# Output projection of 14 groups by Strassen's scheme, with its products behind the attention

## The chip, the cores and the metric
One core of one Trainium2 chip. The metric is the device time of one launch in microseconds; lower is better.

## The reference
```python
mod = (silu(c) @ wmod).reshape(4, 6, 1, -1)          # sa, ca, ga, sb, cb, gb; ga, gb kept away from 0
h = layernorm(x) * (1 + ca) + sa                     # x: 4 x 512 x 1024
q, k, v = rope(h @ wq), rope(h @ wk), h @ wv         # 32 query heads, 8 key heads, each 128
attn = softmax(window_256_causal(q k^T / sqrt(128))) # 4 query heads share a key head
x = x + ga * (attn @ v) @ wo                         # wo: 4096 x 1024
h = layernorm(x) * (1 + cb) + sb
x = x + gb * (sum over the top 2 of 8 experts: w_e * h @ A_e^T @ B_e^T)   # rank 64
```
All of it is float32. A product is made of three matmuls on numbers split in a high and a low part (hi*hi, hi*lo, lo*hi).

## The kernel before, in words
The work is cut into 32 groups n = 8b + g: a batch b of 512 tokens and one key head g with its four query heads. Tokens are taken in four tiles of 128. Phase 0 makes the modulation and the first normalisation, phase 1 the 32 groups, phase 2 the experts. `p1_pe` (L985) writes TensorE's order out by hand. One step of `pe_groups` (L995) does, for the group n-1, the attention (`pe_attention`, L888) and the output projection (`pe_wo`, L816), and then for group n the projections Q0 to Q3 and V (`pe_qv`, L933).

**The attention** goes through 16 units u (tile u // 4, head u % 4). A unit is a product of scores three units ahead, a transposition of the normalised probabilities (`pe_turn`, L859), and filler that covers the softmax on VectorE and ScalarE: one chunk (3 matmuls) of the next group's K at each of u = 0 to 7, and one whole half of the output projection (12 matmuls) behind u = 8, 10, 12 and 15. After u = 5, 9, 13 and the last come the values of a tile (`pe_values`, L867). For the last two tiles they read `vd` and a folded part of `pT`, which GpSimd makes (`pool_group`, L766): five operations for vd and one fold (L783) per unit from 8 on. **The output projection** has 8 halves per group (4 token tiles x 2 column halves of 512), each 4 heads x 3 matmuls; four run in the attention, four behind it. VectorE adds each to `acc` (`dve_wo`, L1261). Then come Q0 to Q3, 24 matmuls of 128x512 each, in banks 1 and 0 by turns; a bank is free when `dve_rope` (L1233) has read it. The rope of K and of each Q takes two copies on ScalarE, three operations on VectorE, a copy on ScalarE and a subtraction on VectorE.

**Batches.** In batch 0 the weights are split in high and low parts and kept in device memory; from batch 1 on SP fetches them (`sp_direct_group`, L533): w_q and w_v of group n once V of n-1 is done, w_k once K is done, w_o once the last half of n-1 is done. In the first four groups of batches 1 and 2 (below: turned groups) a tile of the next batch is normalised besides: statistics, a row stored and broadcast (`sp_turned_row`, L519), two multiplications on VectorE (L1434, L1436), ScalarE's `act_tile` (L1111) and `act_tile_hi`, VectorE's low part (L1447), and the store of both parts (`sp_tile_store`, L528, signals s_hst). These parts lie in the memory of pT, so `act_project` (L1082) ends with ScalarE's wait for that store ahead of the next attention:

```python
if tile is not None:
    eng.wait_ge(s_hst, 32 * (tile + 1))
```
Batch 3 splits the lora weights in its first four groups in the same way. All DMAs that matter here are issued by SP, in program order, onto one queue.

## Time and profile before
| | us |
|---|---|
| runs, lowest / median / highest | 2558.72 / 2559.74 / 2560.05 |
| the profiled execution | 2558.81 |
| its span | 2556.8 |
| TensorE, VectorE, ScalarE, GpSimd busy | 2532.4, 1609.7, 1112.4, 460.2 |
| DMA moved | 504.15 MB |

The span runs from the first to the last instruction; about 2 us of the execution lie around it. Busy times of TensorE overlap, since matmuls are pipelined: the distance from one start to the next says what one costs. The granted TensorE clock is 1.0 of full speed throughout.

### The profile page before, as it was taken

Reading aid. Unit: us, or ns where it says so; the run is one execution under the profiler, and the core shown is the slowest. Engines: PE = TensorE matmul, PEld = TensorE weight load, DVE = VectorE, ACT = ScalarE, POOL = GpSimd, SP = SyncE. Lnnn points to the kernel's source line nnn. Section 1 sums busy time; section 2 is a strip of 40 time slices with the busy share of each in tenths; the row PEclk is TensorE's granted clock in tenths of the full one; section 3 lists DMA queues with packets and bytes.
Section 4 is the critical chain, followed back from the end, with each engine's and each line's share of the span. In section 5 each row is a group of like instructions: output and inputs, shape, how many; then the busy total and the mean of one; then the engine's idle time right before and its main releaser. Section 6 shows DMA issues by size and latency. Waiting matters only on the chain.

```text
span 2556.8 us, 40925 instructions
## 1 busy us (share of the span) xinstructions
PE 2532.4 (99%) x12449; PEld 2101.0 (82%) x12449; DVE 1609.7 (63%) x4594; ACT 1112.4 (44%) x2585; POOL 460.2 (18%) x498
## 2 busy tenths in 40 slices
PE   7999999999999999999999999999999999999999
PEld 4888888887888888888888888888888888887887
DVE  6677776666666665556666665556666665556553
ACT  4555654443445443333445543333333443335441
POOL 0332233332111111102111110111111110101122
PEclk9999999999999999999999999999999999999999
DMA  8766676659445554347444554347554556446221
GB/s 339 280 222 241 246 271 224 244 179 374 171 158 190 199 183 151 117 149 298 167 167 166 197 183 164 137 148 267 189 204 175 203 201 228 180 170 261 101 83 58
DMA packets 160949, 504.15 MB, mean 197 GB/s; under 512 B 17552, under 2 KB 43984, under 8 KB 159312
## 3 DMA queue, kind: packets, MB, share of 16 engines
q1 hardware_dynamic: 156384, 486.65, 52.5%
q10 hardware_dynamic: 4464, 16.25, 1.7%
q8 instruction: 51, 0.84, 0.1%
q14 instruction: 50, 0.41, 0.0%
HBM read 381.17 MB, written 121.68 MB: 197 GB/s over the span
## 4 chain that ended last, share of the span: by engine, by line
PE 95%; DVE 2%; ACT 1%; DMA 1%; issue 1%; DVEq 0%; POOL 0%; ACTq 0%; SPq 0%; POOLq 0%
PE bank L788 30%; PE bank L790 29%; PE bank L789 29%; PE bank L864 4%; PE bank L853 1%; PE bank L1904 1%; PE bank L276 1%; PE bank L905 0%; DMA x1s<-x_scratch 0%; PE bank L303 0%; DMA wm<-in_wmod 0%; ACT w_o_hi L715 0%; PE bank L854 0%; PE bank L1955 0%; DVE qo_lo L1270 0%
## 5 line engine op out<-in xcount | busy, mean ns | idle before, releaser
L788 PE MATMUL bank<-w_o_hi,qo_hi 128*128 128x512 f32 x1024 | 411.4, 402 | 2.0 <-DVE qo_lo L1270 1.5
L790 PE MATMUL bank<-w_o_hi,qo_lo 128*128 128x512 f32 x1024 | 400.4, 391 | 0.0
L788 PE MATMUL bank<-hT_hi,w_q_hi 128*128 128x512 f32 x1024 | 399.5, 390 | 0.2 <-DVE swapped L1242 0.2
L789 PE MATMUL bank<-w_o_lo,qo_hi 128*128 128x512 f32 x1024 | 398.9, 390 | 0.0
L789 PE MATMUL bank<-hT_lo,w_q_hi 128*128 128x512 f32 x1024 | 398.5, 389 | 0.0
L790 PE MATMUL bank<-hT_hi,w_q_lo 128*128 128x512 f32 x1024 | 398.5, 389 | 0.0
L1050 ACT ACTIVATE prob<-prob,nbias 128x256 f32<-128x256 f32 (+1 forms) x512 | 247.3, 483 | 237.8 <-DVE nbias L1289 230.9
L783 POOL TENSOR_TENSOR pT<-pT,lower_t 128x256 fp32r<-128x256 f32 x256 | 196.0, 766 | 475.3 <-DVE pT L1323 475.3
L1241 DVE TENSOR_TENSOR rotated<-bank,cos_t 128x512 f32<-128x512 f32 x160 | 110.6, 692 | 261.8 <-ACT swapped L1035 261.1
L1265 DVE TENSOR_TENSOR acc<-bank,acc 128x512 f32<-128x512 f32 x256 | 173.7, 689 | 160.9 <-PE bank L790 160.8
L772 POOL TENSOR_TENSOR rotated<-v_all 128x256 f32<-128x256 f32 x64 | 48.1, 773 | 1231.5 <-DVE v_all L1329 1231.5
L1034 ACT ACTIVATE swapped<-bank 64x512 f32<-64x512 f32 x160 | 95.4, 596 | 360.4 <-PE bank L790 353.0
L1323 DVE TENSOR_TENSOR pT<-bank,pT 128x256 fp32r<-128x256 f32 (+1 forms) x512 | 195.7, 382 | 85.5 <-ACT pT L1147 85.3
L1147 ACT ACTIVATE pT<-bank 128x256 fp32r<-128x256 f32 (+1 forms) x512 | 177.5, 353 | 155.2 <-PE bank L864 150.2
L790 PEld LDWEIGHTS bank<-w_o_hi,qo_lo 128*128 128x128 f32 x1024 | 192.2, 188 | 42.2
L788 PEld LDWEIGHTS bank<-hT_hi,w_q_hi 128*128 128x128 f32 x1024 | 192.2, 188 | 42.0 <-issue 1.6
L788 PEld LDWEIGHTS bank<-w_o_hi,qo_hi 128*128 128x128 f32 x1024 | 192.3, 188 | 40.1 <-issue 3.2
L790 PEld LDWEIGHTS bank<-hT_hi,w_q_lo 128*128 128x128 f32 x1024 | 192.2, 188 | 40.0
L789 PEld LDWEIGHTS bank<-hT_lo,w_q_hi 128*128 128x128 f32 x1024 | 192.3, 188 | 39.6
L789 PEld LDWEIGHTS bank<-w_o_lo,qo_hi 128*128 128x128 f32 x1024 | 192.8, 188 | 36.7
L1289 DVE CUSTOM_DVE_ANT_0 prob<-bank,mask_t 128x256 f32<-128x256 f32 x384 | 162.4, 423 | 32.8 <-PE bank L864 10.9
L864 PE MATMUL bank<-ident_t,prob 128*128 128x128 f32 x896 | 177.1, 272 | 2.6 <-DVE prob L1299 2.1
(258 smaller groups left out, 4975.4 us busy)
## 6 DMA issues: line engine op xcount, KB each, us to landing
w_q_hi<-w_q_hi_scratch SPq DMA_DIRECT2D x96, 512.0 KB, 8.3
w_q_lo<-w_q_lo_scratch SPq DMA_DIRECT2D x96, 512.0 KB, 8.9
w_o_hi<-w_o_hi_scratch SPq DMA_DIRECT2D x96, 512.0 KB, 7.8
w_o_lo<-w_o_lo_scratch SPq DMA_DIRECT2D x96, 512.0 KB, 8.5
stage<-in_wq SPq DMA_DIRECT2D x32, 512.0 KB, 4.5
stage<-in_wo SPq DMA_DIRECT2D x32, 512.0 KB, 5.3
w_q_hi_scratch<-w_q_hi SPq DMA_DIRECT2D x32, 512.0 KB, 6.3
w_q_lo_scratch<-w_q_lo SPq DMA_DIRECT2D x32, 512.0 KB, 7.2
```

Source lines behind the costliest of these rows:

```text
L783: eng.tensor_tensor(pair[:, :, 2, :], pair[:, :, 0, :].bitcast(F32), lower_t[:].unsqueeze(1).broadcast_to([P, 2, P]), ALU.mult).then_inc(s ...
L788: eng.matmul(o, st[0], mv_[0], start=start, stop=False)
L789: eng.matmul(o, st[0], mv_[1], start=False, stop=False)
L790: return eng.matmul(o, st[1], mv_[0], start=False, stop=stop)
L864: m = eng.transpose(bank[5 + u % 2][:, b * P:(b + 1) * P], prob[:, u % GQ, b * P:(b + 1) * P], ident_t[:])
L1034: eng.activation(swapped[slot][0:half, :], bk[half:HD, :], ACT.Copy)
L1050: eng.activation(tile, tile, ACT.Exp, bias=nbias[:, u:u + 1], scale=-1.0, accum_out=rowsum[:, u:u + 1]).then_inc(s_exp, 1)
L1147: eng.activation(pT[i % 2][0][:, 0:nk, h * P:(h + 1) * P], bank[5 + u % 2][:, 0:nk * P].rearrange("p (b q) -> p b q", q=P), ACT.Copy).then ...
L1241: eng.tensor_tensor(rotated[slot][:], bk[:], cos_t[:], ALU.mult).then_inc(s_dve, 1)
L1265: eng.tensor_tensor(a, wo_bank(half)[:], a, ALU.add).then_inc(s_wor, 1)
L1289: plain(eng.tensor_tensor_reduce(prob[:, u % GQ, 0:w], SBANK[u % 3][:, 0:w], add, -SCALE, FAR, ALU.add, ALU.min, nbias[:, u:u + 1])).then_ ...
L1323: eng.tensor_tensor(lo, bank[5 + u % 2][:, 0:nk * P].rearrange("p (b q) -> p b q", q=P), hi.bitcast(F32), ALU.subtract).then_inc(s_ptl, 1)
```

## The change
In the first seven groups of batches 2 and 3 the output projection is made by Strassen's scheme. Tiles 0 and 1, and tiles 2 and 3, make a pair each. Of a pair the left matrix is 2 x 2 blocks (tile x two heads), the right one 2 x 2 blocks of w_o (two heads x 512 columns). Seven products M1 to M7, each 2 x 3 matmuls of 128x512, take the place of eight. GpSimd and ScalarE make the sums of the left blocks (ten per group, 128x256 each: a sum and a low part on GpSimd, a high part on ScalarE); VectorE adds or subtracts each product to one or two of the outputs (12 per pair). All products stand behind the attention: M3 and M4 of the first pair before its last values, the other twelve after them. In the attention, units 8 to 15 take one chunk each of Q0 of the next group.

The five sums of right blocks that aren't plain blocks of w_o are made once, in batch 1, by GpSimd (`pool_mix`): 28 pieces of 256 columns, each with its raw rows loaded and its two parts (640 KB each) stored by SP (`sp_mix_step`). Their tiles lie where the left sums lie later, so ScalarE waits for all stores before batch 2's attention. SP's fetches go by head (128 columns, pieces of 512 B) and by product, into places of w_q, w_k, w_v and w_o that come free. `plain_part` tiles keep attention outputs unsplit, probability tiles are narrower, and a scratch for DMAs shrinks from 8192 to 512. The diff, cut to its core:

```diff
+PAIRED = 2
+PAIRS = ((0, 1), (2, 3))
+ORDER = (3, 4, 1, 5, 2, 7, 6)
+OUTS = {3: ((0, 1, 1), (1, 1, 1)), 4: ((1, 0, 1), (0, 0, 1)), 1: ((1, 1, 1), (0, 0, 1)), 5: ((0, 1, 1), (0, 0, -1)),
+        2: ((1, 0, 1), (1, 1, -1)), 7: ((0, 0, 1),), 6: ((1, 1, 1),)}
+MIXED = (1, 3, 4, 6, 7)
+PIECES = 4
...
+        def head_slot(h):
+            return {0: (w_q, 0), 1: (w_k, None), 2: (w_q, 0), 3: (w_q, 2)}[h]
+        def mixed_slot(i):
+            return {3: (w_v, None), 4: (w_o, 0), 1: (w_o, 1), 5: (w_o, 2), 2: (w_o, 3), 7: (w_q, 4), 6: (w_q, 6)}[i]
...
+        def sp_enter(eng, n, b, mix=lambda i: None):
+            sp_fetch_qv(eng, n)
+            eng.wait_ge(s_proj, 6 * n + 2)
+            sp_fetch(eng, 5, (n + 1) % KV, s_dk)
+            mix(0)
+            eng.wait_ge(s_wo, wo_at(n, b) + 1)
+            for i in (4, 1, 5, 2):
+                sp_mixed(eng, i, n % KV)
+            mix(1)
+            mix(2)
+            eng.wait_ge(s_proj, 6 * n + 6)
+            sp_head(eng, 0, (n + 1) % KV)
+            sp_head(eng, 3, (n + 1) % KV)
+            for i in (7, 6):
+                sp_mixed(eng, i, n % KV)
+            mix(3)
+            eng.wait_ge(s_proj, 6 * n + 7)
+            sp_mixed(eng, 3, n % KV)
...
+        def sp_paired_group(eng, n, b, leave=False, before_v=lambda: None, before_q3=lambda: None):
+            m = n - 1
+            g = n % KV
+            eng.wait_ge(s_proj, 6 * n + 2)
+            sp_head(eng, 1, g)
+            eng.wait_ge(s_proj, 6 * n + 3)
+            sp_head(eng, 2, g)
+            before_v()
+            done = wo_at(m, b) + 1
+            eng.wait_ge(s_wo, done + len(ORDER) + ORDER.index(3) + 1)
+            sp_fetch(eng, 4, g, s_dv)
+            if leave:
+                eng.wait_ge(s_wo, wo_at(n, b) + 1)
+                for j in range(6, NC):
+                    sp_fetch(eng, j, g, s_do)
+            else:
+                for at, i in enumerate(ORDER):
+                    if i != 3:
+                        eng.wait_ge(s_wo, done + len(ORDER) + at + 1)
+                        sp_mixed(eng, i, g)
+            eng.wait_ge(s_proj, 6 * n + 4)
+                    if i != 3:
+                        eng.wait_ge(s_wo, done + len(ORDER) + at + 1)
+                        sp_mixed(eng, i, g)
...
+            if not leave:
+                eng.wait_ge(s_proj, 6 * n + 5)
+                sp_head(eng, 0, (n + 1) % KV)
+            before_q3()
+            if not leave:
+                eng.wait_ge(s_proj, 6 * n + 6)
+                sp_head(eng, 3, (n + 1) % KV)
+                eng.wait_ge(s_proj, 6 * n + 7)
+                sp_mixed(eng, 3, g)
+        def sp_mix_load(eng, piece):
...
+        def sp_mix(eng, first, pieces):
+            for at in range(len(pieces) - 1):
+                sp_mix_step(eng, first + at, pieces[at], pieces[at + 1])
+        def sp_mix_step(eng, at, piece, following):
+            eng.wait_ge(s_mix, 3 * at + 1)
+            if following is not None:
+                sp_mix_load(eng, following)
+            eng.wait_ge(s_mix, 3 * at + 3)
+            sp_mix_store(eng, piece)
...
+            if b < PAIRED:
+                def piece(i, g0=0):
+                    return g0 + i // PIECES, i % PIECES
+                sp_mix_load(eng, piece(0))
+                for t in range(QT):
+                    n = b * KV + 1 + t
+                    sp_turned_load(eng, b, t)
+                    sp_direct_group(eng, n, b, lambda: sp_turned_row(eng, b, t))
+                    sp_mix(eng, 3 * t, [piece(3 * t + i) for i in range(4)])
+                    sp_tile_store(eng, b, t)
+                with eng.Fori(1 + QT, KV) as g:
+                    sp_direct_group(eng, b * KV + g, b)
+                    sp_mix(eng, 4 * g - 8, [piece(i, g - 2) for i in range(5)])
+                return
...
+            with eng.Fori(1, 1 + QT) as g:
+                pool_group(eng, KV + g - 1)
+                for i in range(3):
+                    pool_mix(eng, 3 * g - 3 + i)
+            with eng.Fori(1 + QT, KV + 1) as g:
+                pool_group(eng, KV + g - 1)
+                for i in range(4):
+                    pool_mix(eng, 4 * g - 8 + i)
...
+        def pool_mix(eng, piece):
+            (b11, b12), (b21, b22) = ((r[:, 0, :], r[:, 1, :]) for r in raw)
+            lo = mix_lo[:].bitcast(F32)
+            eng.wait_ge(s_raw, WS_KEPT + 32 * piece + 32)
+            eng.wait_ge(s_mixd, WS_KEPT + 32 * piece)
+            eng.tensor_tensor(lo[:, 0, :], b11, b22, ALU.add)
+            eng.tensor_tensor(lo[:, 1, :], b12, b22, ALU.subtract)
+            eng.tensor_tensor(lo[:, 2, :], b21, b11, ALU.subtract)
+            eng.tensor_tensor(lo[:, 3, :], b11, b12, ALU.add)
+            eng.tensor_tensor(lo[:, 4, :], b21, b22, ALU.add).then_inc(s_mix, 1)
+            eng.wait_ge(s_mix, 3 * piece + 1)
+            plain(eng.tensor_copy(mix_hi[:], lo)).then_inc(s_mix, 1)
+            eng.wait_ge(s_mix, 3 * piece + 2)
+            eng.tensor_tensor(mix_lo[:], lo, mix_hi[:].bitcast(F32), ALU.subtract).then_inc(s_mix, 1)
...
+        def pe_product(eng, n, b, p, i):
+            t0, t1 = PAIRS[p]
+            if i == 3:
+                eng.wait_ge(s_ol, QT * n + 2 * p + 1)
+                left = sl(qo, lambda q: q[:, 0:2, t0 * P:(t0 + 1) * P])
+            elif i == 4:
+                eng.wait_ge(s_ol, QT * n + 2 * p + 2)
+                left = sl(qo, lambda q: q[:, 2:4, t1 * P:(t1 + 1) * P])
+                left = mixed_sum(p, i)[0:2]
...
+            if i in M_FREE[p]:
+                eng.wait_ge(s_wor, wor_at(n, b) + 1 + M_FREE[p][i])
+            elif p == 1 and i == 3:
+                eng.wait_ge(s_oh, oh_at(n, b) + HIGH_AT[1][22])
...
+                if u < KT:
+                    if u == 0:
+                        eng.wait_ge(s_dk, 32 * (n - (KV - 1)))
+                    m = mm3(eng, bank[0][:], sl(w_k, lambda t: t[:, u, :]), sl(hT, lambda t: t[:, u, :]), u == 0, u == KT - 1)
+                    if u == KT - 1:
+                        m.then_inc(s_proj, 1)
+                else:
+                    if u == KT:
+                        eng.wait_ge(s_dq[0], 32 * (n + 1 - (KV - 1)))
+                    m = pe_head_chunk(eng, 0, u - KT, 1)
+                    if u == UNITS - 1:
+                        m.then_inc(s_proj, 1)
...
+            pe_product(eng, n, b, 0, 3)
+            pe_product(eng, n, b, 0, 4)
+            pe_values(eng, n, b, QT - 1, True)
+        def pe_paired_group(eng, n, b, part=None):
+            pe_paired_attention(eng, n - 1, b)
+            for i in ORDER[2:]:
+                pe_product(eng, n - 1, b, 0, i)
+            for i in ORDER:
...
+            if r == 1 and b is not None:
+                eng.wait_ge(s_wo, wo_at(n, b) + 1)
...
+            if b == PAIRED:
+                eng.wait_ge(s_mixd, WS_KEPT + 32 * PIECES * (KV - 1))
...
+        def dve_product(eng, n, b, p, i):
+            eng.wait_ge(s_wo, wo_at(n, b) + 1 + len(ORDER) * p + ORDER.index(i) + 1)
+            for at, (t, c, sign) in enumerate(OUTS[i]):
+                after = sum_before(i, at)
+                if after:
+                    eng.wait_ge(s_wor, wor_at(n, b) + 1 + 12 * p + after)
+                a = acc[:, PAIRS[p][t], c * 512:(c + 1) * 512]
...
+        def dve_paired_group(eng, n, b, part=None, turned=None, g=None):
+            dve_attention(eng, n - 1, b, tile=turned, paired=True)
+            if turned is not None:
+                dve_turned_chain(eng, turned)
+            for i in ORDER[2:]:
+                dve_product(eng, n - 1, b, 0, i)
+            dve_rope(eng, n, 0)
+            for i in ORDER:
+                dve_product(eng, n - 1, b, 1, i)
             for r in range(1, 1 + GQ):
...
+                if turned is not None and r == 3:
+                    dve_tile_lo(eng, turned)
+                dve_rope(eng, n, r)
...
+                if turned is not None and r == 1:
+                    dve_turned_tile(eng, turned)
+                if g is not None and r == 1:
+                    dve_tile2(eng, g)
+                if g is not None and r in (2, 3):
+                    dve_lora_lo(eng, g, r - 2)
```

## Rows read from the trace of the kernel before
**Rows 1.** The page: busy time by engine, and the chain by engine.
```profile
PE 2532.4 (99%) x12449; PEld 2101.0 (82%) x12449; DVE 1609.7 (63%) x4594; ACT 1112.4 (44%) x2585; POOL 460.2 (18%) x498
...
PE 95%; DVE 2%; ACT 1%; DMA 1%; issue 1%; DVEq 0%; POOL 0%; ACTq 0%; SPq 0%; POOLq 0%
```
**Rows 2.** Waits of TensorE, 800 to 1450 us: total, times, longest.
```profile
PE bank L864 <- DVE prob L1299: 0.4, 1, 0.4
```
**Rows 3.** Timeline of TensorE, the output projection behind an attention: start, duration.
```profile
752.84 0.39 PE L788 MATMUL bank<-w_o_hi,qo_hi 128*128 128x512 f32 x1
...
763.49 0.39 PE L790 MATMUL bank<-w_o_hi,qo_lo 128*128 128x512 f32 x1
```
**Rows 4.** Timeline of TensorE: units 0 and 2, and vd of two attentions.
```profile
719.97 0.27 PE L864 MATMUL bank<-ident_t,prob 128*128 128x128 f32 x1
...
723.22 0.27 PE L864 MATMUL bank<-ident_t,prob 128*128 128x128 f32 x1
...
746.91 0.39 PE L788 MATMUL bank<-pT,vd 128*128 128x512 f32 x1
...
817.95 0.39 PE L788 MATMUL bank<-pT,vd 128*128 128x512 f32 x1
```
**Rows 5.** Groups of GpSimd by line and form: count, busy us, mean ns.
```profile
L720 POOL TENSOR_TENSOR w_q_lo<-stage,w_q_hi 128x1024 fp32r<-128x1024 f32 x28 | 66.7, 2400 | 23.8 <-ACT w_q_hi L715 23.8
...
L774 POOL TENSOR_TENSOR rotated<-rotated 128x256 f32<-128x256 f32 x32 | 23.7, 740 | 2.5
...
L776 POOL CAST vd<-rotated 128x256 fp32r<-128x256 f32 x32 | 12.7, 397 | 4.2
```
**Rows 6.** Timeline of GpSimd in the same group.
```profile
726.77 1.51 POOL L772 TENSOR_TENSOR rotated<-v_all 128x256 f32<-128x256 f32 x2 [46.96 <-DVE v_all L1329]
...
729.71 0.74 POOL L778 TENSOR_TENSOR vd<-rotated,vd 128x256 fp32r<-128x256 f32 x1
...
746.67 0.77 POOL L783 TENSOR_TENSOR pT<-pT,lower_t 128x256 fp32r<-128x256 f32 x1 [0.87 <-DVE pT L1323]
...
750.13 0.73 POOL L783 TENSOR_TENSOR pT<-pT,lower_t 128x256 fp32r<-128x256 f32 x1 [0.19 <-DVE pT L1323]
```
**Rows 7.** Timeline of SP's DMA issues in the same group.
```profile
763.91 0.33 SPq L508 DMA_DIRECT2D w_o_hi<-w_o_hi_scratch  x1
...
767.60 0.47 SPq L508 DMA_DIRECT2D w_o_lo<-w_o_lo_scratch  x1
782.66 0.53 SPq L531 DMA_DIRECT2D hT_hi_scratch<-l_hi  x1
783.23 0.68 SPq L531 DMA_DIRECT2D hT_lo_scratch<-l_lo  x1
```
**Rows 8.** DMA issues: count, KB each, median us to landing.
```profile
hT_lo_scratch<-l_lo SPq DMA_DIRECT2D x12, 512.0 KB, 5.6
...
lora_a_lo_scratch<-l_lo SPq DMA_DIRECT2D x2, 512.0 KB, 3.6
```
**Rows 9.** Stretches of 2 us; last columns: clock, DMA share, GB/s.
```profile
775.00:777.00 2.00, 2.00 (x10) 1.65 (x10) 0.94 (x2) 1.01 (x2) 0.00 (x0) 1.00 0.95 385
777.00:779.00 2.00, 2.00 (x11) 1.65 (x10) 1.27 (x3) 0.89 (x2) 0.00 (x0) 1.00 0.04 14
```
**Rows 10.** Timeline of ScalarE: the exponential of unit 2.
```profile
790.54 0.40 ACT L1050 ACTIVATE prob<-prob,nbias 128x128 f32<-128x128 f32 x1 [0.47 <-DVE nbias L1289]
```
**Rows 11.** Timeline of VectorE: the rope of K, and two sums.
```profile
755.52 0.69 DVE L1241 TENSOR_TENSOR rotated<-bank,cos_t 128x512 f32<-128x512 f32 x1
...
758.23 0.69 DVE L1257 TENSOR_TENSOR kt_all<-rotated,kt_all 128x512 fp32r<-128x512 f32 x1 [0.70 <-ACT kt_all L1044]
758.84 1.28 DVE L1265 TENSOR_TENSOR acc<-bank,acc 128x512 f32<-128x512 f32 x2
```
**Rows 12.** Timeline of TensorE in the opening: idle time before in brackets.
```profile
12.70 1.94 PE L303 MATMUL bank<-wm,cT 128*32 128x512 f32 x8 [6.12 <-DMA wm<-in_wmod]
...
27.75 1.93 PE L303 MATMUL bank<-wm,cT 128*32 128x512 f32 x16
```

More of the change, by code:

```diff
@@ new lines, in sp_mix_load, with sp_mix_store @@
+        def sp_mix_load(eng, piece):
+            g, jc = (piece[0], piece[1])
+            j, half = divmod(jc, 2)
+            for y in range(2):
+                rows = wo[bass.ds(g * GQ * HD + (j + 2 * y) * HD, HD), :].rearrange("p (c s n) -> p c s n", c=2, s=2)[:, :, half, :]
+                eng.dma_start(raw[y][:], rows).then_inc(s_raw, 16)
+        def sp_mix_store(eng, piece):
+            g, jc = piece
+            j, half = divmod(jc, 2)
+            for z, tile in enumerate((mix_hi, mix_lo)):
+                to = w_s[z][bass.ds(g * P, P), :].rearrange("p (i j s n) -> p i j s n", i=len(MIXED), j=2, s=2)[:, :, j, half, :]
+                eng.dma_start(to, tile[:].bitcast(F32)).then_inc(s_mixd, 16)
@@ L626, in x_tile @@
+            for g in range(1 + QT, KV):
+                n = b * KV + g
+                q = g - QT
+                sp_paired_group(eng, n, b, g == KV - 1, (lambda: sp_part(eng, q, n)) if not store and q < 3 else lambda: None)
+                if not store and q == 1:
+                    sp_store_gate(eng, 1, part_row)
         def x_tile(b, t):
@@ L992, in p1_pe @@
             pe_groups(eng, last, False)
-            pe_attention(eng, GROUPS - 1, (), True, late=True)
+            pe_attention(eng, GROUPS - 1, last, (), True, late=True)
         def pe_groups(eng, b, ln, direct=True):
-            with eng.Fori(1, 1 + QT) as g:
-                n = b * KV + g
-                pe_attention(eng, n - 1, K_AT, direct, o_direct=direct)
-                for half in range(FILL, 8):
-                    pe_wo(eng, n - 1, half, direct)
-                pe_qv(eng, n, direct, b * QT + g - 1 if ln and not direct else None)
-                if ln and not direct:
-                    eng.wait_ge(s_laf, b * QT + g + 1)
@@ L1496, in dve_groups @@
                 i = b * QT + g - 1
-                turned = ln and not split
+                turned = not split
                 dve_attention(eng, n - 1, b, late_v=not split, tile=i if turned else None, split=split)
```

478 lines of the change are left out of this document (339 added, 139 removed).

## The prediction, as it stood before the result
> **What bounds the kernel now.** I read the page first: TensorE is busy 99% of the span and holds 95% of the chain that ended last [rows 1]. Busy time alone says little of pipelined matmuls, so the waits of TensorE come next: in 650 us of the second and third batch its longest total wait is 0.4 us [rows 2]. It never waits; the pace of its instructions is the time. Of the output projection, 48 matmuls of 128x512 run from 752.84 until Q0 starts behind 763.49, 10.88 us or 0.227 us each [rows 3]. A group repeats after 71.04 us (the vd matmul at 746.91 and 817.95) [rows 4]. So a matmul taken out is worth 0.227 us, as long as nothing new makes TensorE wait. GpSimd idles 47 us between groups [rows 6].
>
> **The change, part by part.**
> *Matmuls removed.* A plain output projection has 8 halves x 4 heads x 3 = 96 matmuls; 14 products x 2 x 3 = 84. Twelve fewer in each of 14 groups (the first seven of batches 2 and 3): 168 x 0.227 = 38.1 us off the path.
>
> *The mixing in batch 1.* GpSimd computes 28 pieces of mixed weights once, 3 in each of its first four groups, 4 in each of the last four. A piece is five operations of 128x256 (0.74 us each), a cast and a subtraction of 128x1280. From 2.40 us at 1024 columns and 0.74 at 256 the subtraction is 2.95 with a fixed part of 0.19. The cast, 0.40 at 256, lies between 1.2 (with the same fixed part) and 2.0 (in proportion); I take 1.5 [rows 5]. A piece is 8.4 us (8.1 to 8.9). The work, 34 us of four pieces, would fit GpSimd's 47 us. What doesn't fit is the hand-over: each piece waits until both stores of the one before have landed, and SP issues these stores only behind the group's fetch of w_o. In absolute times of one turned group:
> - SP issues w_o from 763.91 to 768.07 [rows 7]; the DMA engines are full with it until 777 (share 0.95, then 0.04) [rows 9]. The first piece, ready since its last fold at 750.13 plus 9 [rows 6], is stored behind it: with 1.31 MB and 0.52 MB of raw rows at the 385 GB/s of that row and some slower writing, 783 (781.6 to 784).
> - A store of 1.31 MB by itself: the pair of tile stores takes 0.6 us from first to second issue [rows 7] and 5.6 to land, the lora pair lands in 3.6, each pair 1.05 MB [rows 8]. With 2 us fixed, a quarter more bytes: 4.5 to 7.2, and I take 6.3.
> - Second piece 791.4, stored 797.7, third 806.1. Only then does SP issue the tile's own store, behind the third piece's: 2.36 MB, 9.9 us (8.7 to 11.4), landed at 816.0.
> ScalarE waits for that store (s_hst, since the tile lies in pT) before the next attention. Before, its store was issued at 782.66 and landed by 788.8 [rows 7, 8], and its exponential of unit 2 ran at 790.54 [rows 10]: the old slack was 1.7 us. From ScalarE's release to TensorE's third transposition are an exponential, an evacuation, a subtraction and a normalisation, 1.5 us: 817.5 against 794.3 (723.22 + 71.04) [rows 4]. TensorE stands 23.2 us, four times: **92.8** (73 to 110).
> - In groups without a tile the fourth piece is the late one: stored 812.4, done 820.8, then the next group's vd (726.77 to 730.45, 3.7 us [rows 6]) and four folds, 3.1: 827.6 against 817.95 [rows 4, 6]. 9.6 us, three times: **28.8** (11 to 42).
> - At the entry to batch 2 ScalarE waits for all 28 stores. From the last fold (30.9 after the attention's start, plus 9.6) four pieces and four stores, one of them behind 4 MB, take 60.4: 100.9 where 80.2 was due; TensorE stands **18.5** (10 to 25).
> Sum of the mixing: 140 us (94 to 177).
>
> *The clock.* After its 6.1 us of idling in the opening, 8 matmuls took 1.94 us, where 16 take 1.93 later [rows 12]: TensorE comes out of an idle stretch at half pace (the granted column says 1.00 there, so I go by the pace). Eight long stands follow here; for each I take 1 us (0 to 5, a third of the 15 us between the two rows): **8**. The Trainium skill (TensorE: Matmul & The Clock Gate, Part 1) says the default state is throttled at 1.2 GHz and only activity releases it; the row agrees.
>
> *The paired group.* TensorE's filler in the attention is K and Q0, 3 matmuls at each of 16 units; its total there falls, and units with 3 fillers ran without waits before, so nothing is charged. VectorE sums 24 outputs instead of 8 (0.61 us each by their spacing, two in 1.28 [rows 11]), 9.8 us more, nearly all behind the attention. Counted from the last transposition: TensorE makes its 14 products and the values by 21.2, Q1 by 26.7, Q2 by 32.2, Q3 by 37.6. VectorE waits for the last flat part (6.4), sums the first pair until 12.3, ropes K (755.52 to 758.84, 3.3 us [rows 11]) until 15.7, sums the second pair until 23.0 and ropes Q0 until 26.4. Q2 needs bank 1 at 26.7 and has it at 24.9. GpSimd's part of each product is ready 2 us or more ahead (three lows of the second pair at 11.9 to 14.2, needed from 14.4 on). So plain groups only just pass: 0.3 us each. In the four turned groups of batch 2 the tile's two multiplications (2.5 us) now stand behind Q0's rope, ScalarE's tile work behind them, and Q1's copies behind that: Q3's bank is free at 33.3 instead of 32.2, and rope 3 ends at 42.0 with the attention due at 43.6. Rope 3's end to the attention's start was 5.1 us before, so it starts at 46.9: 3.3 us, four times. Together **16** (0 to 34).
>
> *DMA.* A paired group fetches 13 MB instead of 10, heads in pieces of 512 B. The nearest deadline is K's, issued at 27.7 behind 8 MB that began at 13, needed at 43.6; at 385 GB/s it lands by 37. Cost nothing, cover 6 us; without it K's chunk stands at each attention's head.
>
> **Sum**, against the profiled execution (2558.8 us, span 2556.8, the median of the runs 0.9 above): 2558.8 - 38.1 + 140 + 8 + 16 = 2685 us. With all bounds at once 2615 and 2772; as they don't fall together, 2625 to 2735.
>
> **The rivals.**
> 1. *The mixing is hidden, the kernel gets faster.* The hand-over takes so little that the tile's store still lands by 791. It has to be issued by 783 then, so two stores and two pieces must pass in the 15 us behind 768, where the two pieces alone take 16.8. Against it are both rows of GpSimd and of stores [rows 5, 8]; for it is only that the gate isn't where I read it in the code, or that GpSimd is much faster on these forms. That gives 2558.8 - 38.1 + 16 = 2537 us, and it decides from the point where a piece with its store takes 7.5 us instead of 14.7.
> 2. *The store overtakes the fetch.* If writes need not wait behind 4 MB of reads, the first piece is stored at 774: 9 us off each chain, so 14 x 4, 0.3 x 3 and some 12 at the entry: 69 instead of 140, 2614 us. For it speaks that nothing orders the two but the queue; against it, that the engines have no free share until 777 [rows 9].
> 3. *VectorE becomes the bound in all 14 groups.* Its margins in the plain group are 1.8 us; if sums out of PSUM beside GpSimd's doubled work lag by a few per cent, each group loses some 4 us: 14 x 4 instead of 16, 2725 us. GpSimd's folds take 0.77 beside a busy VectorE and 0.73 without [rows 6], which says little contention. The Trainium skill (GPSIMD Engine Reference, the table of its interfaces) says that GpSimd shares its SBUF ports with VectorE and contends where a VectorE instruction has two SBUF inputs; the row agrees in size, at 5%.
> 4. *The tile's store is not the gate*, because a landing of it after ScalarE's need stops less than I charge: the mixing then costs the fourth pieces and the entry alone, 47 us instead of 140, 2592 us. No row of before shows this wait as a loss, which leaves it open.
>
> **How the numbers follow.** Forecast 0.62; rival 1, 0.08; rival 2, 0.11; rival 3, 0.12; rival 4, 0.07. The predicted time is 2685. From 2605 to 2735 lie the forecast, rival 2 and most of rival 3; outside remain rivals 1 and 4 and the top of rival 3, under 2 in 10. A measurement here can tell 0.2%, 5 us, from no change. Faster 0.08 (rival 1), the same 0.02, slower 0.90.
>
> **What would show it.** In the changed profile the page's 40 slices should show TensorE below 9 tenths in slices 11 to 20 only. ScalarE should wait for a DMA (hT scratch from l_lo) four times, 25 us each, ahead of its exponential; TensorE's fourth to sixth late attention should wait for GpSimd's fold of pT or vd. GpSimd's casts of 128x1280 should take 1.2 to 2.0 us. The period of a plain paired group should be 68.6 us, of a turned one 71.6. I am wrong in the main point if attentions 9 to 12 start 71 us apart, and in the paired part if their period is over 72.

## The result and the profile after

The changed kernel takes 2776.2 us (median of 4 runs, 2775.1 to 2778.4) where the kernel before takes 2559.5: ratio 1.0848, 95% interval 1.0829 to 1.0867. It is slower by 217 us; I had said 126, and the range ended at 2735.

The page of the changed kernel: busy time by engine, TensorE's busy tenths and its granted clock in 40 slices of 69 us, and the chain by engine [rows 1]:

```profile
PE 2546.4 (92%) x12281; PEld 2095.7 (76%) x12281; DVE 1824.9 (66%) x4818; ACT 1168.5 (42%) x2781; POOL 896.4 (32%) x974
...
PE   7999999999697679885969999999999999999999
...
PEclk9999999999898889997989999999999999999999
...
PE 66%; issue 9%; DMA 7%; DVE 7%; POOL 6%; ACT 3%; SPq 2%; DVEq 0%; POOLq 0%; ACTq 0%
```

The 168 matmuls are gone (12281 instead of 12449). After the opening TensorE is below 9 tenths in slices 11, 13 to 15, 17 to 19 and 21, which is batch 1 and the entry to batch 2; I had said 11 to 20, so it reaches one slice further. Its share of the chain fell from 95% to 66%. Its waits over the whole run (total, times, longest), where there was 0.4 us in a quarter of the time [rows 2]:

```profile
PE bank L1243 <- DVE prob L1727: 146.4, 28, 24.7
PE bank L1079 <- DMA hT_lo<-hT_lo_scratch: 28.9, 1, 28.9
PE bank L1079 <- DVE swapped L1647: 10.2, 7, 2.1
```

"DVE prob" only names the last link. ScalarE's waits in 640 to 1120 us tell what held it, four times some 22.5 us, as forecast (25):

```profile
ACT prob L1426 <- DMA hT_lo_scratch<-l_lo: 90.2, 4, 22.9
```

One turned group of the changed kernel, on SP's queue, GpSimd and TensorE (start, duration, idle before) [rows 6, 7]; w_o is issued from 694.69:

```profile
699.04 1.20 SPq L756 DMA_DIRECT2D raw<-in_wo  x2
700.29 0.85 SPq L764 DMA_DIRECT2D w_s_hi_scratch<-mix_hi  x1
701.18 4.74 SPq L764 DMA_DIRECT2D w_s_lo_scratch<-mix_lo  x1
...
736.66 0.59 SPq L764 DMA_DIRECT2D w_s_hi_scratch<-mix_hi  x1
737.29 0.65 SPq L764 DMA_DIRECT2D w_s_lo_scratch<-mix_lo  x1
737.98 1.36 SPq L592 DMA_DIRECT2D hT_hi_scratch<-l_hi  x1
739.39 1.48 SPq L592 DMA_DIRECT2D hT_lo_scratch<-l_lo  x1
```
```profile
713.92 0.74 POOL L972 TENSOR_TENSOR mix_lo<-raw 128x256 f32<-128x256 f32 x1 [26.64 <-DMA w_s_lo_scratch<-mix_lo]
...
728.81 0.73 POOL L972 TENSOR_TENSOR mix_lo<-raw 128x256 f32<-128x256 f32 x1 [5.62 <-DMA w_s_lo_scratch<-mix_lo]
```
```profile
748.35 0.48 PE L1243 MATMUL bank<-ident_t,prob 128*128 128x128 f32 x1 [17.83 <-DVE prob L1727]
...
751.60 0.77 PE L1079 MATMUL bank<-hT_hi,w_k_hi 128*128 128x512 f32 x1
752.17 0.63 PE L1080 MATMUL bank<-hT_lo,w_k_hi 128*128 128x512 f32 x1
752.60 0.60 PE L1081 MATMUL bank<-hT_hi,w_k_lo 128*128 128x512 f32 x1
```

The first piece's store has landed 19.2 us behind w_o's first issue (predicted 19.1), a store takes 5.6 us (6.3), and the tile's store comes last. TensorE stands 17.8 us, and behind it three matmuls of 512 columns start 0.57 and 0.43 us apart where they ran at 0.227 [rows 3]. The granted clock of these stretches (third column from the end) is the lower of its two levels, 1.2 of 2.4 GHz, and is back at the upper one from 754 us:

```profile
748.00:750.00 2.00, 1.65 (x6) 1.43 (x7) 1.87 (x12) 1.76 (x8) 0.00 (x0) 0.50 1.04 397
750.00:752.00 2.00, 2.00 (x8) 1.77 (x7) 0.34 (x2) 0.81 (x4) 0.00 (x0) 0.50 0.97 309
754.00:756.00 2.00, 2.00 (x13) 1.69 (x12) 1.89 (x10) 1.14 (x5) 1.79 (x4) 1.00 1.03 420
```

Where the 217 us are, by the distance of a fixed event from group to group (ScalarE's first copy of V), in us:

| groups | before | after | more in all | in my sum |
|---|---|---|---|---|
| 9 to 12, turned | 71.1 | 97.1, 100.4, 98.6, 98.3 | 110 | 97 with the clock |
| 13 to 15 | 71.0 | 75.9, 82.8, 82.0 | 28 | 32 with the clock |
| 16, entry to batch 2 | 73.1 | 134.0 | 61 | 19.5 with the clock |
| 17 to 31, paired | 70.8 to 75.3 | 75.0 and three times 72.7 for the turned, 69.2 to 78.8 for the others | 19 | -22 |

### The profile page after: what moved, and what is told of

The parts are those of the page before. It is cut to its first block, busy times and chain, and to the rows that moved or that the text cites. A ratio compares the mean times of both kernels' runs of the same rounds, so it can differ in the third digit from the quotient of the medians.

```text
span 2773.3 us, 42764 instructions
## 1 busy us (share of the span) xinstructions
PE 2546.4 (92%) x12281; PEld 2095.7 (76%) x12281; DVE 1824.9 (66%) x4818; ACT 1168.5 (42%) x2781; POOL 896.4 (32%) x974
## 4 chain that ended last, share of the span: by engine, by line
PE 66%; issue 9%; DMA 7%; DVE 7%; POOL 6%; ACT 3%; SPq 2%; DVEq 0%; POOLq 0%; ACTq 0%
PE bank L1079 20%; PE bank L1081 20%; PE bank L1080 20%; DMA raw<-in_wo 3%; PE bank L1243 3%; POOL mix_lo L980 1%; DVE acc L1686 1%; DMA hT_lo_scratch<-l_lo 1%; SPq L569 1%; DVE swapped L1647 1%; DVE rotated L1650 1%; POOL mix_hi L978 1%; POOL mix_lo L973 1%; POOL mix_lo L976 1%; POOL mix_lo L974 1%
## 5 line engine op out<-in xcount | busy, mean ns | idle before, releaser
L1081 PE MATMUL bank<-hT_hi,w_q_lo 128*128 128x512 f32 x912 | 357.1, 392 | 0.0
L1080 PE MATMUL bank<-hT_lo,w_q_hi 128*128 128x512 f32 x912 | 356.7, 391 | 0.0
L1079 PE MATMUL bank<-w_o_hi,qo_hi 128*128 128x512 f32 x744 | 299.3, 402 | 11.3 <-DVE acc L1670 9.3
L1081 PE MATMUL bank<-w_o_hi,qo_lo 128*128 128x512 f32 x744 | 291.5, 392 | 0.0
L1080 PE MATMUL bank<-w_o_lo,qo_hi 128*128 128x512 f32 x744 | 290.9, 391 | 0.0
L1243 PEld LDWEIGHTS bank<-ident_t,prob 128*128 128x128 f32 x896 | 123.3, 143 | 186.7 <-DVE prob L1727 165.0
L1420 ACT ACTIVATE qo_hi<-rotated 128x512 fp32r<-128x512 f32 x128 | 80.9, 632 | 335.7 <-DVE rotated L1650 335.6
L1686 DVE TENSOR_TENSOR acc<-acc,bank 128x512 f32<-128x512 f32 x336 | 208.4, 681 | 17.9 <-PE bank L1081 15.6
L1079 PE MATMUL bank<-hT_hi,w_k_hi 128*128 128x512 f32 x368 | 170.2, 462 | 29.4 <-DMA hT_lo<-hT_lo_scratch 28.9
L1727 DVE TENSOR_SCALAR prob<-prob,rrow 128x256 f32<-128x256 f32 (+1 forms) x512 | 195.0, 386 | 0.2 <-issue 0.2
```

The costliest lines, as they stand in the source:

```text
L1079: eng.matmul(o, st[0], mv_[0], start=start, stop=False)
L1080: eng.matmul(o, st[0], mv_[1], start=False, stop=False)
L1081: return eng.matmul(o, st[1], mv_[0], start=False, stop=stop)
L1243: m = eng.transpose(bank[5 + u % 2][:, b * P:(b + 1) * P], prob[:, u % GQ, b * P:(b + 1) * P], ident_t[:])
L1686: eng.tensor_tensor(a, a, M_BANK[p][i][:], ALU.add if sign > 0 else ALU.subtract).then_inc(s_wor, 1)
L1727: plain(eng.tensor_scalar(tile, tile, rrow[:, u:u + 1], None, ALU.mult)).then_inc(s_nrm[u % GQ], 1)
```

## The experiments

**First round: the order of SP's queue, and the paired part alone.** The first run changes two lines of `sp_groups`, the second also moves the reload:

```diff
-                    sp_mix(eng, 3 * t, [piece(3 * t + i) for i in range(4)])
                     sp_tile_store(eng, b, t)
+                    sp_mix(eng, 3 * t, [piece(3 * t + i) for i in range(4)])
```

> The tile's store is issued ahead of the three pieces in the four turned groups of batch 1; all else as in the changed kernel. Theory 1 (the order on SP's queue): ScalarE's wait for hT scratch in those groups goes, and with it the stand of TensorE and the half clock behind it; groups 9 to 12 fall from 97 to 100 us to 72 to 77, the whole from 2776 to 2670 to 2700 us. Rival (contention: the pieces slow VectorE's tile and the queue, whatever the order): the four groups stay above 88 us and the whole above 2735 us.

Measured 2740.5 us, 36 less: above 2735, as the rival had it, but with one of its four groups far below 88, so neither forecast held whole. Group 9 fell to 75.3 us, but 10 to 12 stayed at 92. ScalarE's wait for the tile's store is gone; VectorE's waits in 740 to 1000 us show the next one:

```profile
DVE stats L1839 <- DMA stage<-in_x: 50.9, 3, 17.7
```

The first piece now waits for the tile, so the third is stored at 840.17, and the next tile's rows and the next Q and V are issued behind it, with V done at 821. The same fault, one load further on.

```diff
@@ sp_groups, the last group of batch 1
+                sp_mix(eng, 4 * g - 8, last[0:2])
+                sp_reload(eng, b + 1)
+                sp_mix(eng, 4 * g - 7, last[1:5])
```

> As the kernel before in this list, and the reload of hT for batch 2 is issued ahead of the last three pieces of the last group of batch 1. Theory 1 (SP's order again: the reload stood behind the pieces): TensorE's wait of 28.9 us for hT_lo goes, so 25 to 33 us less than the tile's store first alone. Rival (the entry is set by the stores of the last pieces, for which ScalarE waits before its first softmax copy of batch 2): the wait moves there and 0 to 8 us are won.

Measured 2728.9 us: 11.6 less, of which the entry gave 9.4 (134.3 to 124.9). That lies between the two forecasts (25 to 33, and 0 to 8), nearer to the rival's. TensorE no longer waits for hT, but ScalarE waits longer for the last pieces' stores, 33.5 us where it was 28.9 without this move:

```profile
ACT prob L1433 <- DMA w_s_lo_scratch<-mix_lo: 33.5, 1, 33.5
```

In the changed kernel TensorE stands at the entry twice, 28.9 us for hT and then 24.7 us for the probabilities behind ScalarE's wait. With the first stand taken away the second grows to 30.8.

> The changed kernel with the tile's store and the next tile's load both ahead of the pieces in the turned groups. Theory (with the store alone first, VectorE waited 16.3 us for the tile's rows, since their load stood behind the last piece): that wait goes, groups 10 to 12 fall from 92 to 76 to 84 us, the whole from 2740 to 2690 to 2715 us. Rival (the late vd and the late fetches of Q and V behind the third piece set them): they stay above 88 us.

```diff
                     sp_tile_store(eng, b, t)
+                    if t < QT - 1:
+                        sp_turned_load(eng, b, t + 1)
                     sp_mix(eng, 3 * t, [piece(3 * t + i) for i in range(4)])
```

(Against the first run's kernel; tile 0's rows are loaded ahead of the loop.)

Measured 2703.4 us: the theory held. Groups 10 to 12 take 80 to 81 us, and VectorE's wait for the rows is gone.

> Leaves the mixing of weights out (no piece, no raw load, no store of mixed weights); the five mixed tiles are fetched with the same bytes from the plain output weights, so the output is not the reference's. What is left is the paired part alone. Theory 1 (the trace of after: paired groups 17 to 31 sum to +19 us against before): 2567 to 2587 us, so slower than before even with the mixing for nothing. Rival (my prediction's terms, -38 + 8 + 16): 2535 to 2550 us.

Measured 2585.8 us (ratio 1.0100, 1.0084 to 1.0117). The theory held, the rival didn't: with the mixing for nothing the change still costs 26.5 us. Groups 9 to 16 are as before to 0.1 us, so all of it lies in batches 2 and 3: groups 21 and 22 take 75.5 and 77.4 us, 23 takes 70.5, and 25 to 29 take 72.2 to 80.2, against 68.6 in my sum (29 took 75.3 before).

> All 28 pieces are kept, four in each of the seven groups of batch 1 and none behind the entry: the first step of SP ahead of the wait for the output projection (GpSimd is idle there from its last fold), the second behind it, the tile's store, the third, and the fourth behind the next group's first fetches; the reload is ahead of the last step. Theory 1 (order alone): within 0 to 20 us of the kernel without mixing. Rival (GpSimd's fourth piece holds vd and so the attention in every group, 4 to 11 us each): 30 to 80 us above it.

```diff
-                    sp_direct_group(eng, n, b, lambda: sp_turned_row(eng, b, t))
-                    sp_mix(eng, 3 * t, [piece(3 * t + i) for i in range(4)])
+                    sp_fetch_qv(eng, n)
+                    if t:
+                        step(t - 1, 3)
+                    sp_fetch_ko(eng, n, b, lambda: (step(t, 0), sp_turned_row(eng, b, t)))
+                    step(t, 1)
                     sp_tile_store(eng, b, t)
+                    step(t, 2)
```

(The groups behind the fourth tile, the entry and GpSimd's order change in the same sense.) Measured 2642.7 us, 133.5 less than the changed kernel, and 57 above the kernel without mixing: the rival's number, but not its cause, for in batch 1 TensorE has no wait for GpSimd. The entry takes 78.1 us. But groups 9 to 12 still take 82 us and 13 to 15 take 75. TensorE waits for a DMA only 3.1 us; its waits for prob are 23.6 us in nine pieces over all of batch 1. VectorE waits for the turned row 28.9 us in four (the run of the row first, below, asks what that is worth), and its own time grew.

**Second round: why the spread pieces cost.**

> As the spread kernel with all its raw loads and mixed stores, but GpSimd's seven operations of each piece are three memsets of one column, so the mixed weights are zeros and the output is not the reference's. Theory (contention: beside GpSimd's pieces VectorE's operations with both operands in SBUF take 1.43 instead of 0.69 us and so on): plain groups 13 to 15 fall from 75 to 71 to 72 us and the turned groups from 82 to 72 to 76 us, the whole from 2643 to 2590 to 2605 us. Rival (the traffic of the pieces): it stays above 2625 us.

```diff
-            eng.tensor_tensor(lo[:, 0, :], b11, b22, ALU.add)
...
-            eng.tensor_tensor(mix_lo[:], lo, mix_hi[:].bitcast(F32), ALU.subtract).then_inc(s_mix, 1)
+            plain(eng.memset(mix_lo[:, 0, 1:2].bitcast(F32), 0.0)).then_inc(s_mix, 1)
```

Measured 2577.2 us, 65.5 less than with the arithmetic, and groups 9 to 15 back at 70.9 to 71.1. The theory's mechanism held; the result lies 13 us below the range that it gave. The loads and stores of all pieces cost nothing in batch 1; what costs is GpSimd's arithmetic. From the first V of batch 1 to that of batch 2, first the spread kernel, then the one with the transfers alone (length; busy time of TensorE, its weight loads, VectorE, ScalarE, GpSimd; clock, DMA share, GB/s):

```profile
653.33:1284.47 631.14, 591.50 (x2747) 488.76 (x2746) 427.22 (x1065) 238.08 (x602) 307.52 (x301) 0.97 0.70 244
653.80:1224.40 570.60, 569.65 (x2747) 478.17 (x2746) 359.79 (x1065) 239.00 (x602) 87.55 (x189) 1.00 0.77 270
```

The stretch is 60.5 us shorter, and VectorE's 1065 instructions take 67.4 us less. TensorE's busy time falls by 22 us of these, the clock rising from 0.97 to 1.00, so the clock's share is in the price of the arithmetic. VectorE's groups by form in 740 to 1210 us (count, busy, mean ns), first the spread kernel, then the one with the transfers alone:

```profile
L1655 DVE TENSOR_TENSOR rotated<-rotated,swapped 128x512 f32<-128x512 f32 x30 | 39.2, 1306 | 1.0
L1732 DVE TENSOR_SCALAR prob<-prob,rrow 128x256 f32<-128x256 f32 x73 | 37.7, 517 | 0.0
L1675 DVE TENSOR_TENSOR acc<-bank,acc 128x512 f32<-128x512 f32 x48 | 31.9, 686 | 20.2 <-PE bank L1086 20.1
L1652 DVE TENSOR_TENSOR swapped<-swapped,sin_t 128x512 f32<-128x512 f32 x30 | 29.8, 992 | 0.0
```
```profile
L1671 DVE TENSOR_TENSOR acc<-bank,acc 128x512 f32<-128x512 f32 x55 | 37.3, 689 | 37.5 <-PE bank L1082 37.5
L1728 DVE TENSOR_SCALAR prob<-prob,rrow 128x256 f32<-128x256 f32 x76 | 26.9, 354 | 0.0
L1651 DVE TENSOR_TENSOR rotated<-rotated,swapped 128x512 f32<-128x512 f32 x33 | 22.8, 692 | 1.1
L1648 DVE TENSOR_TENSOR swapped<-swapped,sin_t 128x512 f32<-128x512 f32 x33 | 22.5, 681 | 0.0
```

This run by itself also makes GpSimd early, but the spread kernel's TensorE had no wait for GpSimd to lose. A sum of two SBUF tiles takes 1306 ns instead of 692 on average, the scaling of a tile in SBUF 517 instead of 354, and a sum with one operand in PSUM the same 686 and 689. The Trainium skill (GPSIMD Engine Reference, 8. Key points) names two classes of VectorE instruction that contend with GpSimd, those with two SBUF inputs and those in a two-port mode, of which the scaling would be one. The runs agree in what grew and what didn't, and add the size on average in this stretch: 1.9 times for the sum, 1.5 for the product with the sine table (992 for 681) and for the scaling. The averages hide two kinds. In the spread kernel a sum of VectorE that meets nothing of GpSimd's takes 0.69 us; one that begins inside GpSimd's subtraction of 1280 columns takes 3.25 to 3.32, as long as that subtraction:

```profile
788.00 0.69 DVE L1655 TENSOR_TENSOR rotated<-rotated,swapped 128x512 f32<-128x512 f32 x1
```
```profile
805.38 3.31 POOL L985 TENSOR_TENSOR mix_lo<-mix_lo,mix_hi 128x1280 fp32r<-128x1280 f32 x1
805.99 3.25 DVE L1655 TENSOR_TENSOR rotated<-rotated,swapped 128x512 f32<-128x512 f32 x1
```

It ends 0.55 us behind the subtraction: it all but waits for the whole of it, and the profile shows the wait as its duration. Beside GpSimd's sums of 256 columns (0.74 to 1.2 us) the same sum takes 1.1. So the price hangs on how long GpSimd's operations are; to cut the subtraction into narrow ones was not tried.

> As the spread kernel, but in the four turned groups the turned row's round trip is issued ahead of the first piece's step instead of behind it. Theory (VectorE's waits for stage from ln_scratch, up to 7.8 us, came from that order): these waits fall to about 2 us and groups 9 to 12 by 3 to 5 us each, 12 to 20 us in all. Rival (contention of GpSimd and VectorE sets the turned groups): the waits fall and the groups keep 80 us or more.

```diff
-                    sp_fetch_ko(eng, n, b, lambda: (step(t, 0), sp_turned_row(eng, b, t)))
+                    sp_fetch_ko(eng, n, b, lambda: (sp_turned_row(eng, b, t), step(t, 0)))
```

Measured 2643.9 us, nothing: the rival held. VectorE's wait for the row falls from 28.9 us in four to 11.1 in four, and groups 9 to 12 take 82 to 84 us all the same.

> The whole computation as the best whole kernel, with the fourth piece of a group behind the next group's vd and ahead of its folds instead of ahead of vd (the last group's stays ahead, for ScalarE waits for its store); so the third piece and the fourth lie less in the turn from V to the attention, where TensorE stood 4.5 us for prob. Theory (the contention costs where VectorE has no slack, at that turn): groups 10 to 12 fall from 81 to 82 us to 76 to 79, groups 13 to 15 from 75 to 77 us to 72 to 74, the whole from 2602 to 2570 to 2588 us, still above before. Rival (VectorE loses the same wherever the pieces lie, or the folds come late): 2596 us or more.

```diff
+                pool_vd(eng, KV + g - 1, 0)
+                pool_mix(eng, 4 * g - 5)
+                for u in range(UNITS - FOLDED, UNITS):
+                    pool_fold(eng, KV + g - 1, u)
-                pool_group(eng, KV + g - 1)
-                for i in range(4):
+                for i in range(3):
                     pool_mix(eng, 4 * g - 4 + i)
```

SP's fourth step moves with it, behind the fetch of K. Measured 2598.6 us against 2601.7 of the same kernel without this move (below): 3 us, and the rival held. Groups 9 to 12 take 80 to 82 us, 13 to 15 take 74.5 to 76: the cost stays when the piece moves. Less arithmetic on GpSimd, or shorter operations, are left to try; no run did.

The kernel without mixing isn't the exact floor for the rest: the one with the transfers alone is 8.6 us faster (2577.2 against 2585.8), all of it in groups 17 to 31, where both run the same instructions. There the changed kernel and the spread kernel lose 19 us against before, the one with the transfers alone 20 and the one without mixing 29. So the transfers alone are the better floor and the arithmetic costs 65.5 us. Why the other is slower (it fetches its mixed tiles from the places of the plain weights) was not tried.

**Second round: why the paired part loses.**

> The kernel without mixing (output not the reference's), with the fetch of the next head 0 issued behind the stores of LoRA, tile and modulation instead of ahead of them, and the modulation's store ahead of the last two fetches of its group. Theory (in batch 3 ScalarE waits for these stores, which stand behind the mixed fetches): TensorE's waits of 3.1, 3.1, 2.6, 3.2 and 5.8 us in groups 25 to 29 shrink to under 1.5 us each, the whole falls by 8 to 16 us. Rival (the stores only come as late as VectorE makes their data): 0 to 3 us.

```diff
-            if not leave:
-                eng.wait_ge(s_proj, 6 * n + 5)
-                sp_head(eng, 0, (n + 1) % KV)
             before_q3()
             if not leave:
                 eng.wait_ge(s_proj, 6 * n + 6)
+                sp_head(eng, 0, (n + 1) % KV)
+                before_head3()
                 sp_head(eng, 3, (n + 1) % KV)
```

Measured 2561.6 us, 24.2 less than the kernel without mixing: the theory held, by more than I gave it. ScalarE's waits for a DMA in batch 3, first without and then with the move:

```profile
ACT prob L1416 <- DMA lora_a_lo_scratch<-r_lo: 12.3, 2, 6.2
ACT prob L1416 <- DMA lora_b_lo_scratch<-r_lo: 11.9, 2, 6.2
ACT prob L1416 <- DMA mod_scratch<-lf: 8.4, 1, 8.4
```
```profile
ACT prob L1414 <- DMA lora_b_lo_scratch<-r_lo: 4.6, 2, 2.5
ACT prob L1414 <- DMA lora_a_lo_scratch<-r_lo: 2.7, 1, 2.7
ACT prob L1414 <- DMA mod_scratch<-lf: 1.3, 1, 1.3
```

Groups 25 to 28, which took 72.2 to 74.2 us, take 68.4 to 69.2, what my sum gave for a plain paired group (68.6).

> The kernel without mixing, with VectorE's three plain paired groups of batch 2 written out one behind the other instead of a hardware loop; no instruction is added, so the weights are again the plain ones and the output is not the reference's. Theory (VectorE's 4 us stands put down to issue are its loop's seam: code that is not there yet behind the jump): the two stands and TensorE's 6.1 and 6.4 us for prob go, periods of groups 21 and 22 fall from 75.5 and 77.4 to 69 to 71 us, the whole from 2586 to 2572 to 2578 us. Rival (something else stops VectorE there, as the full DMA): the stands stay and the whole is within 2 us of the kernel without mixing.

```diff
-                    with eng.Fori(1 + QT, KV) as g:
+                    for g in range(1 + QT, KV):
                         dve_paired_group(eng, b * KV + g, b)
```

Measured 2569.9 us, 15.8 less than the kernel without mixing: the theory held, a little beyond its range. Groups 21 to 23 take 68.5, 68.6 and 68.4 us. In the loop, VectorE's timeline at the seams had stood for no data (the kernel of the stores first, groups 21 and 22):

```profile
1588.00 0.29 DVE L1701 TENSOR_TENSOR prob<-bank,mask_t 128x128 f32<-128x128 f32 x1 [6.00 <-issue]
1591.43 0.29 DVE L1703 CUSTOM_DVE_ANT_0 prob<-bank,prob 128x128 f32<-128x128 f32 x1 [3.13 <-issue]
...
1666.69 0.29 DVE L1701 TENSOR_TENSOR prob<-bank,mask_t 128x128 f32<-128x128 f32 x1 [5.65 <-issue]
1670.19 0.29 DVE L1703 CUSTOM_DVE_ANT_0 prob<-bank,prob 128x128 f32<-128x128 f32 x1 [3.20 <-issue]
```

Why this loop and none of the others, two last runs asked:

```diff
                 if ln:
+                    for i in range(64):      # and 128
+                        plain(eng.memset(beside_kt[:, i % P:i % P + 1], 0.0))
                     with eng.Fori(1 + QT, KV) as g:
```

> The kernel of the stores first (no mixing, output not the reference's), VectorE's plain groups of batch 2 in their hardware loop, with 64 memsets of one column ahead of that loop, so the loop lies 64 instructions later in the program. Theory (code that isn't there: what matters is where the loop lies): VectorE's stands put down to issue at the seam to group 22 (5.65 and 3.20 us) change place, or go; the group's period changes from 78.8 us by 3 or more. Rival (something of the loop's own, or of the moment): both stands stay, the period is within 1 us of 78.8. Group 21 also bears the memsets' own time, some 4 to 7 us.

> As the run before in this list with 128 memsets. Theory (the loop's place in the program): the stands differ again from those with 64 and from those without; the period of group 22 may be 69 to 80 us. Rival: 78.8 within 1 us, as with 0 and 64.

With 64 instructions ahead of the loop the stands are gone: groups 21 to 23 take 68.4, 68.6 and 68.4 us, the whole 2544.4 us (one run), 17 less than without them. With 128 (one run) they are back, group 22 takes 78.6 us, the whole is 2565.6, 4 more, of which group 20, where the memsets stand, has 3.5. VectorE's lines read much as before the shift:

```profile
1669.91 0.29 DVE L1701 TENSOR_TENSOR prob<-bank,mask_t 128x128 f32<-128x128 f32 x1 [6.37 <-issue]
1673.40 0.29 DVE L1703 CUSTOM_DVE_ANT_0 prob<-bank,prob 128x128 f32<-128x128 f32 x1 [3.20 <-issue]
```

So nothing in the loop itself makes the stands, nor the number of its passes; the likeliest cause is where the loop lies in the program. That the memsets merely delay VectorE is hardly it, for twice as many bring the stands back, but no run shifts the loop without delaying it. The first theory held for 64; for 128 it had said that the stands would differ from those without a shift, and they don't: there the rival held. The Trainium skill (Advanced Engine Details and Errata, ISA Cache) gives an engine two lines of 256 instructions each; a loop that touches a third line would have to fetch at its seam. That is a guess: no row here shows a line being fetched or how many instructions the loop has, and why the third pass through the loop has no stand stays open.

**Third round: do the parts add?**

> The kernel without mixing (output not the reference's) with both repairs, VectorE's groups written out and the stores of batch 3 ahead of head 0. Theory (the parts add): 2586 - 16 - 24 = 2546 us, 2541 to 2550, so below before by 10 to 17 us: what my sum gave for the paired part (-38 + 8 + 16 = -14). Rival: the two repairs share a wait and it stays within 5 us of before.

Both repairs on the kernel without mixing. Measured 2541.5 us in 5 runs, ratio 0.9931 (0.9917 to 0.9945): the paired part alone wins 17.6 us, where the sum had 22. Its page:

```profile
PE 2502.6 (98%) x12281; PEld 2069.3 (81%) x12281; DVE 1753.2 (69%) x4818; ACT 1170.3 (46%) x2781; POOL 667.8 (26%) x778
```

> The whole computation: the spread kernel with VectorE's plain groups of batch 2 written out and the stores of batch 3 ahead of head 0. Theory (the parts add): 2643 - 16 - 24 = 2603 us, 2597 to 2610, still slower than before, since the contention of GpSimd's pieces with VectorE (some 60 us) is larger than all that the paired part can win. Rival (they overlap, the same waits): above 2612 us.

The spread kernel with both repairs, which computes everything. Measured 2601.7 us, ratio 1.0167 (1.0152 to 1.0183): the parts add to 1 us. It is 175 us faster than the changed kernel and 43 slower than the one before. With the fourth piece moved (above) it is 2598.6, ratio 1.0155 (1.0138 to 1.0172), the best whole kernel of the study; neither beats before.

## Why the prediction was wrong, step by step

The sum had 126 us, the chip gave 217. The runs cut the 217 in three, by differences of medians, in this order (with the arithmetic taken out first the parts might come out otherwise; no run did that):

| part | in the sum | measured | from |
|---|---|---|---|
| hand-over of the pieces on SP's queue, with its clock | 148 | 133.5 | changed kernel less spread kernel |
| GpSimd's arithmetic beside VectorE | 0 | 65.5 | spread kernel less transfers alone |
| the paired part | -22 | 18 | transfers alone less before (26.5 by the kernel without mixing) |

- **The gate of the mixing was right, its prices partly by luck.** ScalarE's four waits for hT scratch and the first store at 19.2 us came as written. A cast took 1.25 us and a subtraction 2.95, a piece alone 7.95 (I took 8.4, though its terms as written add to 8.15). Rivals 1, 2 and 4 fell with it. In whole groups 9 to 12 TensorE is idle 23.4 us a group, as charged (23.2); of these 17.8 to 18.8 are the stand behind the tile's store, up to 3.5 are waits for prob ahead of it, and 1.9 is a wait for a sum of VectorE. But the order on SP's queue gives back only 66 us there (394 to 328 in the spread kernel) where I charged 97, 16 of 32 in groups 13 to 15, and 56 at the entry where I charged 19.5. That these add to 138 beside my 148 is luck. So are the 28 us of groups 13 to 15 beside 28.8: TensorE waits there for GpSimd's fold twice, 4.3 us each, and in group 13 not at all, where I had 9.6 three times; 12 us of the 28 stay in the spread kernel, where nothing waits for GpSimd.
- **The clock was too small.** I took 1 us for a stand, 8 in all. Here are whole groups 9 to 12 and the entry, first the changed kernel, then before (busy time of TensorE, ...; the granted clock is the third column from the end):

```profile
653.16:1047.52 394.36, 300.80 (x1372) 249.49 (x1371) 215.90 (x556) 132.22 (x326) 136.55 (x136) 0.88 0.53 185
1288.18:1422.14 133.96, 77.07 (x350) 62.80 (x349) 61.99 (x135) 26.15 (x72) 61.76 (x54) 0.79 0.76 269
```
```profile
653.49:937.73 284.24, 284.24 (x1373) 239.12 (x1373) 187.07 (x556) 133.43 (x325) 38.02 (x52) 1.00 0.51 175
1150.67:1223.81 73.14, 72.73 (x347) 60.75 (x348) 50.04 (x134) 26.06 (x71) 13.03 (x14) 1.00 0.70 263
```

  The same work keeps TensorE busy 75.2 us a group instead of 71.1: 4.1 us lost to pace, of which 3.6 come from the stretches below full clock (busy time there, times what the granted clock lacks). The clock falls behind some of the short waits too (0.50 from 825.35 us, behind 2.75 us of idling) and not only behind the long stand. With groups 13 to 15 (3.2 each) and the entry (4.3) that is some 30 us instead of 8. The bound I kept, 5 us a stand, covered it; the value I took from a row of the opening didn't.
- **The entry, 18.5 us, was 61.** I charged the last pieces' stores (how 18.5 follows from the 100.9 against 80.2 I did not write down) and forgot who else stands in SP's queue behind a step of mixing: the reload of hT. TensorE stood 28.9 us for it and then 24.7 behind the stores. Moving the reload alone won 9.4, since the stores then held longer; to have the pieces early took away 56.
- **The step that failed most is in rival 3**: "GpSimd's folds take 0.77 beside a busy VectorE and 0.73 without, which says little contention". That row is GpSimd's. The cost falls on VectorE, whose SBUF sum went from 0.69 to 1.3 us on average (3.3 at most), while GpSimd's own operations mostly kept their 0.74 (some of its sums took 1.19). I read the price on the wrong engine, and charged it to batches 2 and 3 only, while most of GpSimd's new work is in batch 1, where the price came to 65.5 us. What I cite there of the Trainium skill gives no size, so there was nothing for the row to agree with. The trace of before had it: in batch 0, where GpSimd splits weights (2400 ns each [rows 5]), VectorE's rope product took 779 ns, in batch 1 it took 682, and the scaling 393 and 354; the sum of two SBUF tiles kept its 692, so the sign was a weak one. Here are both stretches, 80 to 580 and 720 to 1220 us of before:

```profile
L1242 DVE TENSOR_TENSOR swapped<-swapped,sin_t 128x512 f32<-128x512 f32 x35 | 27.3, 779 | 0.0
```
```profile
L1242 DVE TENSOR_TENSOR swapped<-swapped,sin_t 128x512 f32<-128x512 f32 x35 | 23.9, 682 | 0.0
```

- **The paired group's own working held**: 3.3 us of waits in a turned group are 3.3 by TensorE's waits in groups 18 and 19 (2.3 and 1.0). Its period is 72.7 us, 71.6 in the sum, so 1.1 us is none of these waits; the first one, 75.0, runs partly below full clock. A plain one takes 68.4 to 69.2 once both repairs are in (68.6). What I missed is beside it. In batch 3 I costed DMA at nothing with a cover of 6 us for K's fetch, and looked at no store: the lora and modulation stores stand behind the mixed fetches, and ScalarE waits for them, 24 us. And a loop that costs 16 us by its place in the program, as it seems, is a term that no row of before could give; its nearest sign there is idle time put down to issue, at most 1.3 us in this phase.
- Why the stands of the loop came only in its first two passes is not settled, nor whether the stands of 1.2 us put down to issue in every group have the same cause. Neither was tried.

## What to carry to other kernels

Before you give an idle GpSimd work, cost what that does to VectorE: find VectorE's operations that work on SBUF alone (here the sums of two tiles and the scalings) and that will run beside it, and charge each that meets a GpSimd operation with up to the whole length of that one; idle time of one of the two engines is not free time. When a step with its own wait goes into a queue written by hand, list everything queued behind it, up to the end of the next stage, and not only the consumer that you have in mind: in this case the next tile's rows and the reload of hT, and the stores of the pieces, the tile, the lora weights and the modulation, each took a turn as the gate. And when a time changes by ten or more microseconds with no wait that names data, look for idle time put down to issue at a loop's seam, and shift the loop before you explain anything else.

## What the runs showed of the hardware that was not expected

- GpSimd beside VectorE, on average: 1306 for 692 ns (two SBUF inputs), 992 for 681, 517 for 354 (scaling in SBUF), 686 for 689 with an operand in PSUM. A single sum is 3.3 us long when it meets GpSimd's subtraction of 3.3 us, and 0.69 when it meets nothing. 28 pieces of 8 us cost 65.5 us of the whole, 60.5 of them in batch 1.
- The transfers of all pieces, 51 MB (599.7 less 548.3), cost nothing once they stand nowhere in the way: groups 9 to 15 take 70.9 to 71.1 us with a DMA share of 0.77, 0.50 before.
- The same loop, shifted by 64 instructions: 17 us less; by 128: 4 us more (one run each).
- The issue of a piece's second store on SP took 4.74 us close behind w_o's eight fetches, where it took 0.65 for the next two pieces. So SP itself stood, and with it what it does next.
- Of TensorE's four waits of 1.9 us in groups 9 to 12 the granted clock fell to 0.50 behind one (791.4 to 793.3 us) and stayed at 1.00 behind the three others.
